# Twelve unread fp32 products per chunk in the waits of TensorE in the scan of layer 0

## The reference, cut to what matters

```python
def step(carry, xs):
    W_in, W_out = carry
    q_t, k_t, v_t, lr_t = xs
    k_h = softmax(einsum('blhd,bDhd->blhD', k_t, W_in)) * lr_t[..., 1:]
    q_h = softmax(einsum('blhd,bDhd->blhD', q_t, W_in))
    qk = einsum('bqhD,bkhD->bhqk', q_h, k_h) * mask
    o_t = einsum('bqhD,bDhd->bqhd', q_h, W_out) + einsum('bhqk,bkhd->bqhd', qk, v_t)
    W_out = W_out + einsum('bnhD,bnhd->bDhd', k_h, v_t)
    for _ in range(2):
        g_out = -attn(W_in, k_t, v_t)
        g_in = -attn(W_out, v_t, k_t)
        W_in, W_out = W_in - lr_in * g_in, W_out - lr_out * g_out
    return (W_in, W_out), o_t
```

## Time and profile before

| | |
|---|---|
| profiled execution | 961.6 us, span 959.9 us, mean granted TensorE clock 0.798 |
| median of the runs | 961.51 us |
| TensorE products busy | 664.2 us (69%) |
| TensorE weight loads busy | 507.6 us (53%) |
| VectorE busy | 646.2 us (67%) |
| ScalarE busy | 341.3 us (36%) |
| GpSimd busy | 373.1 us (39%) |

### The profile page before, as it was taken

How to read it: one execution, slowest core, us unless ns; L and a number is a source line. 1 busy time by engine, 2 the same in 40 slices (tenths; PEclk the granted TensorE clock), 3 DMA queues, 4 the chain that set the end, 5 groups by cost and what they waited for, 6 DMA issues and landing times. The chain is left out here.

```text
span 959.9 us, 19158 instructions
## 1 busy us (share of the span) xinstructions
PE 664.2 (69%) x6868; PEld 507.6 (53%) x6876; DVE 646.2 (67%) x1830; ACT 341.3 (36%) x782; POOL 373.1 (39%) x513
## 2 busy tenths in 40 slices
PE   1677787778857556899999983166687723596674
PEld 1266565556635444777777782144565612265453
DVE  3763788878867582877777843855546647894895
ACT  1664111111111254576666531212134413452331
POOL 1450344444440544356555046427416630030231
PEclk9978656655569595999999998567889965888995
DMA  2000000000000400030000234254375332000000
GB/s 53 1 1 10 4 2 2 3 2 3 2 3 1 77 0 5 24 95 10 8 6 11 70 108 143 62 87 135 93 201 161 121 113 56 1 1 1 5 22 16
DMA packets 66287, 41.24 MB, mean 43 GB/s; under 512 B 11888, under 2 KB 64192, under 8 KB 66208
## 3 DMA queue, kind: packets, MB, share of 16 engines
q1 hardware_dynamic: 62432, 32.43, 13.9%
q0 software_dynamic: 3776, 7.78, 2.3%
HBM read 26.72 MB, written 13.47 MB: 42 GB/s over the span
## 5 line engine op out<-in xcount | busy, mean ns | idle before, releaser
L1733 ACT ACTIVATE l1a_weights<-l1a_score,l1a_low_top 128x128 f32<-128x128 f32 (+1 forms) x256 | 90.2, 424 | 38.1 <-DVE l1a_low_top L1765 34.3
L1765 DVE TENSOR_REDUCE l1a_low_top<-l1a_score 128x2 f32<-128x512 f32 (+1 forms) x96 | 66.1, 688 | 53.2 <-PE l1a_score L1642 32.9
L1597 POOL TENSOR_TENSOR l1a_q_of<-l1a_q_rows,l_quad_of 128x1024 fp32r<-128x1024 f32 x32 | 59.8, 1893 | 37.9 <-ACT l1a_q_rows L1722 37.9
L1788 DVE COPY l1a_weightsT<-l1a_flip 128x512 f32<-128x512 f32 x96 | 65.4, 681 | 0.8 <-PE l1a_flip L1677 0.7
L1639 PE MATMUL l1a_score<-l1a_k_rows,l1a_q_of 128*128 128x128 f32 (+1 forms) x256 | 53.2, 313 | 18.0 <-ACT l1a_weights L1733 10.3
L1277 POOL DMA_INDIRECT l_done<-l2e_done,l2r_rows x47 | 45.1, 959 | 44.6 <-DVE l2e_done L2480 44.0
L1677 PE MATMUL l1a_flip<-eye,l1a_weights 128*128 128x128 f32 x384 | 59.2, 278 | 0.8 <-ACT l1a_weights L1733 0.2
L1639 PEld LDWEIGHTS l1a_score<-l1a_k_rows,l1a_q_of 128*128 128x128 f32 x256 | 38.4, 201 | 33.0 <-ACT l1a_weights L1733 20.4
L1677 PEld LDWEIGHTS l1a_flip<-eye,l1a_weights 128*128 128x128 f32 x384 | 47.3, 145 | 3.1 <-issue 0.8
L827 POOL TENSOR_TENSOR l0s_shared<-l0s_own,l0s_grown 128x512 f32<-128x512 f32 x16 | 18.1, 1134 | 76.2 <-ACT l0s_grown L817 76.2
L1260 POOL DMA_INDIRECT l_rows<-l2r_sent,l2r_slot x32 | 30.9, 967 | 28.7 <-DVE l2r_slot L1244 16.0
(11 more groups left out here) (528 smaller groups left out, 1944.5 us busy)
## 6 DMA issues: line engine op xcount, KB each, us to landing
l2e_wgu<-in_l_wgu SPq DMA_DIRECT2D x47, 128.0 KB, 2.1
l1e_w<-in_l_w SPq DMA_DIRECT2D x46, 128.0 KB, 2.2
l_rows<-l2r_rows SPq DMA_DIRECT2D x1, 3055.0 KB, 18.2
l2e_wd<-in_l_wd SPq DMA_DIRECT2D x47, 64.0 KB, 1.9
l2r_rows<-l_rows SPq DMA_DIRECT2D x3, 780.0 KB, 7.4
l2e_mixed<-l_done SPq DMA_DIRECT2D x8, 256.0 KB, 4.9
l_rows<-l1r_rows SPq DMA_DIRECT2D x1, 1483.5 KB, 11.8
l1r_rows<-l_rows SPq DMA_DIRECT2D x3, 387.0 KB, 4.2
```

Of the source, the lines that this page charges most:

```text
L1597: nc.gpsimd.tensor_tensor(q_of[i][:, 4 * g:4 * g + 4, :], rep(q_rows[:, g, :], 1, 4), rep(lat.quad_of[:, 0, 0:4], 2, L), ALU.mult).then_in ...
L1733: last = nc.scalar.activation(weights[s % 2][:, n * width:(n + 1) * width], score[s % 2][:, n * width:(n + 1) * width], ACT.Exp, bias=low_ ...
L1765: nc.vector.tensor_reduce(low_top[:, s % 2, 0:len(heads)], score[s % 2][:, :].rearrange("p (h k) -> p h k", k=key_tiles * P), AX.X, ALU.ma ...
L1788: nc.vector.tensor_copy(weightsT[s % 4][:, :], flip[s % 2][:, :]).then_inc(moved, 1)
```

## The change

A helper `fill` issues products of the identity with the first 128 columns of the normed input, both fp32, into a part of a PSUM bank that nobody reads: columns 384 to 511 of `grown_ps`, or of `out_ps`. Per chunk there are 2 before the wait for `here_ready` (chunks 1 to 15, with a wait for the copy out of `grown_ps` ahead of them), 2 before `ready["own"]`, 2 before `ready["out"]`, 2 before `old_ready`, and 4 before `ready["in"]` (chunks 0 to 14). Nothing else is changed.

```diff
+                def fill(count, bank=grown_ps):
+
+                    for _ in range(count):
+                        nc.tensor.matmul(bank[:, 3 * P:4 * P], core.eye[:, :], core.xnT[:, 0:P], start=True, stop=True)
...
                 for c in range(NCK):
                     if c:
+                        pe.wait_ge(grown_kept, c)
+                        fill(2)
                         pe.wait_ge(here_ready, c)
...
                         give_results(c - 1)
+                    fill(2)
                     pe.wait_ge(ready["own"], c + 1)
                     last = add(OLD, 2, fast.v_toks, c, both(own[c % 2][:, 0, :, :].rearrange("p (g h) i -> p g (h i)", g=2)))
+                    fill(2)
                     pe.wait_ge(ready["out"], c + 1)
...
                     last.then_inc(out_summed, 1)
+                    fill(2)
                     pe.wait_ge(old_ready, c + 1)
...
                     if c < LAST:
+                        fill(4, out_ps)
                         pe.wait_ge(ready["in"], c + 1)
                         add(MID, 2, fast.k_toks, c, lambda rows, g: by_tokens_in[rows, 0:3:2, g, :]).then_inc(in_summed, 1)
```

## The result

The changed kernel takes 969.47 us (median of five runs, 968.07 to 972.83) against 961.86 us before: ratio 1.0089, 95% interval 1.0063 to 1.0114. It is slower by 7.6 us; 5.8 us faster was forecast, and the range ended at 960.5.

The account below looks back on a forecast made before the run. It took the scan as bound by VectorE's chain, with waits for TensorE at 1.2 GHz. Savings of 9.1 us less 3.3 for four falls gave net 5.8: 961.6 to 955.8 us, range 951.5 to 960.5.

Parts of the forecast that it names:

- The clock rises and holds mostly: In the scan: clock rises within the first chunk, mean from 0.61 to 0.9 or more, falling about four times.
- `w_here` to `top_own`, -2.0 us: This stretch takes 1.01 instead of 1.21 us in the 10 chunks at the low clock, saving 2.0 us.
- `w_here` no longer waits, -4.5 us: VectorE's wait for TensorE at `w_here` vanishes: 10 times 0.45 us, saving 4.5 us.
- `top_in`, -1.6 us: VectorE's wait for TensorE at `top_in` shrinks by 0.12 us in 14 chunks, saving 1.6 us.
- `top_own` to `w_old`, 0: VectorE's chain here takes 5.81 us at either clock level; fills fit the pauses at the high clock and cost 0.
- The falls, 3.3 us: Four drops to 1.2 GHz in the scan, each losing 0.3 to 1.3 us, taken as 0.8; 3.3 us lost.
- The last chunk, -1.0 us: GpSimd's last sum gets the copy of the wide product sooner, saving 1.0 us.
- The price of a fill: TensorE time for two or four added products: 0.46 or 0.92 us at high clock, 0.85 or 1.7 at low.
- 9.1 us if all is high: Total saving in the scan if the clock stayed high throughout, before subtracting the falls.
- Rivals 3 and 4: Low spell at every chunk's end, 974 us, chance 0.06; low clock stays throughout the scan, about 1000 us, chance 0.04.
- rival 3: Low spell always ends the chunk, so four products delay `w_here` by 1.1 us; 13 us, 974 us, chance 0.06.

Follow-up runs that it names:

- gpsimd_after_copy: The changed kernel with GpSimd's 128x512 product also waiting for VectorE's predicated copy of the same chunk; 963.13 us, ratio 1.0013 to the kernel before.
- held_four_before_old: The changed kernel with GpSimd held until the predicated copy is done, and four instead of two products before `old_ready`; 955.06 us, ratio 0.9905 to the kernel before.
- memset_beside_copy: The kernel before, no products added, plus a GpSimd memset of 128x1120 fp32 placed to start ahead of VectorE's predicated copy; 985.57 us, ratio 1.0242.
- no_inner_fill: The changed kernel without the four products before `ready["in"]`, the other eight kept; 990.42 us, ratio 1.0305 to the kernel before.
- four_before_old: The changed kernel with four instead of two products before `old_ready`, GpSimd not held; 971.85 us, ratio 1.009 to the kernel before.

## Why the prediction was wrong

Its steps, with the sums over the scan in the two profiles:

- **The clock rises and holds mostly**: right, 0.87; after its first rise at 105.2 us it fell seven times in the first 15 chunks, and once more in the last, instead of four times. Wrong in a detail that cost: a fall was taken to last one short spell, since TensorE would have no pause; two lasted 10.2 us with TensorE busy throughout.
- **`w_here` to `top_own`, -2.0 us**: right, 17.12 to 15.19 us.
- **`w_here` no longer waits, -4.5 us**: this step failed. From `top_in` to `w_here` the 15 chunks take 61.5 us instead of 56.0: +5.5 where -4.5 was forecast, a miss of 10 us. One reason stands in the paragraph on the pauses: "The fills run beside VectorE's work; no engine but TensorE has an instruction more". True, but an instruction of GpSimd moved. The wide product's end was booked as 0.85 us sooner and as room for the fill; that GpSimd was waiting for its copy in every chunk (76.2 us in 16 times on the page, 4.03 in the earlier trace rows), and what its earlier start would meet, was not followed. Against the 3.43 us of a chunk without either, the ten chunks with a held copy (3.90 to 4.18) are 6.5 us over, and the five in which the inner fill met 1.2 GHz (4.00 to 4.34) the other 3.6. The hold stood in no term; the fill's delay did, among the falls.
- **`top_in`, -1.6 us**: 1.20 instead of 1.31 us at the high clock, as taken (0.12). Three chunks with 1.74 at the low clock (0, 5 and 11) bring the sum to +0.3.
- **`top_own` to `w_old`, 0**: +2.8 us. Chunks 5 and 11 take 7.31 instead of 5.81, chunk 0 5.61 instead of 4.84; chunk 1 is 0.8 shorter. The price that the prediction gave for an always low clock (+1.15 to 1.2 here, 2.6 us a chunk) was somewhat small (1.5; chunk 5 in all 2.1 above its neighbour); it was then counted as 0.3 to 1.3 a fall.
- **The falls, 3.3 us**: mis-sized. Against the scan of the prediction with the clock high throughout they cost 3.6 before `w_here`, 2.8 before `w_old`, 1.9 before `top_in` and 1.0 in the last chunk, 9.3 us. This and the 6.5 of the held copy are the whole miss. By these sums the held copy alone would have left the kernel 0.7 us slower (6.5 less 5.8) and the falls alone 0.2 (9.3 less 9.1). The second fits `gpsimd_after_copy`, which is level with the kernel before. The two are not quite apart: with GpSimd held the long spells were gone as well, and why is open.
- **The last chunk, -1.0 us**: 0. The clock fell at about 286.1 us, before the wide product.
- **The price of a fill**: at the high clock, 0.46 us for two and 0.92 for four, near enough. The rows are 0.71 and 1.05 us long with the last record's whole 0.28 us in them, the weight loads of two take 0.52 us, and no `w_old` or `w_here` is late by them there. At the low clock it was too small: 0.85 for two, and 1.15 measured (from 157.72 to the start of the next add at 158.87). The price had been taken from the 512-column product, which has one weight load for four times the columns.
- **9.1 us if all is high**: borne out by `held_four_before_old`, whose scan is 8.8 us shorter (194.74 to 185.98) with GpSimd held besides.
- **Slips that change nothing**: four falls at 0.8 are 3.2 us, 14 times 0.12 is 1.7, and 1.06 less 0.85 is 0.21, not 0.17. VectorE waited for TensorE at a fourth place before, `w_old`, once, 0.7 us. ScalarE does read columns 384 to 511 of `grown_ps`, but only after the wide product has overwritten what the fills left.

Together 5.5 + 2.8 + 0.3 - 1.9 = +6.7 us, as the scan grew (194.74 to 201.46). What is left of the 7.6 is within the runs' spread. The profiled execution is the slowest of the five, 972.83 us: of its 11.2 us above the profile before, 6.7 lie in the scan and 2.1 in the finish of the layer, begun at 1.2 GHz; the rest lies in the later stages and is not traced to a cause.

None of the rivals was this one. Rivals 3 and 4 had the sign. What rival 3 describes, the inner fill at 1.2 GHz in front of `w_here`, came in five of 15 chunks, with waits of 0.57 to 0.91 us. No rival had the held copy: the list asked what the fills do to TensorE and not what a faster TensorE sets free.

## What to carry to other kernels

When a stage gets faster, go through the instructions that it releases, not only the ones that waited longest: for each, write down when it will start now and which instruction of the engine next to it will be under way. An instruction of GpSimd that starts just before one of VectorE can hold it until its own end; here an order that 0.09 us kept was lost. A wait that fixes the order cost nothing measurable where it only restored the order there was. In this loop the unread products paid only with 14 a chunk and GpSimd held: with less the clock fell, and they were then themselves late; eight were worse than twelve or none.

## What the runs showed of the hardware

- The predicated copy of 128x128 takes 0.30 us, and 1.06 us if a 128x512 product of GpSimd (1.13 us) starts 0.23 us before it (the changed kernel). A GpSimd memset, which reads nothing, holds a one-input fp32 instruction of VectorE as well, 1.13 instead of 0.22 us (`memset_beside_copy`).
- TensorE can be busy for 26.15 of 27 us, with eight unread fp32 products a chunk between the narrow ones, and stay at 1.2 GHz (`no_inner_fill`). With twelve the spells were 3.4, 6.8 or 10.2 us long (the changed kernel). With 14, four of them before `old_ready`, and GpSimd held, it stayed at 2.4 GHz for 174 us (`held_four_before_old`); without the hold two spells of 10.2 us came back (`four_before_old`).
